# Reordering the slots and the prologue of a fused cross-attention and FP6 layer

## The reference, cut to what matters

```python
# x, ctx: (32, 256, 512) fp32; 16 heads of 32 columns; a causal mask
q = layernorm(x) @ w_q.T + b_q;  k = ctx @ w_k.T + b_k;  v = ctx @ w_v.T + b_v
scores = (q . k) / sqrt(32), -inf above the diagonal
attn = softmax(scores)
x = x + tanh(g_xattn[0]) * ((attn . v) @ w_o.T + b_o)
d = FP6(layernorm(x)), each block of 32 scaled by max|.| / 7.5; w_f likewise
out = x + tanh(g_ffn[0]) * (d @ w_f.T + b_f)
```

## Time and profile before

| | |
|---|---|
| time, median of 3 runs | 1438.02 us (1437.79 to 1441.76) |
| the profiled execution | 1438.69 us, span 1436.9 us |
| TensorE busy | 1361.0 us, 95% |
| VectorE, ScalarE, GpSimd busy | 75%, 69%, 68% |
| mean granted clock of TensorE | 0.986 |
| matmuls | 10333 |

### The profile page before, as it was taken

One profiled execution on the slowest core, in us unless ns is written; L12 is line 12 of the kernel. 1 busy time (PEld: TensorE's weight loads), 2 busy tenths in 40 slices (PEclk: granted clock), 3 DMA queues, 4 the chain that ended last, 5 costly groups with the idle time before them and its releaser, 6 DMA issues.

```text
span 1436.9 us, 33559 instructions
## 1 busy us (share of the span) xinstructions
PE 1361.0 (95%) x10333; PEld 1190.9 (83%) x10333; DVE 1075.8 (75%) x3802; ACT 984.3 (69%) x3101; POOL 975.6 (68%) x1170
## 2 busy tenths in 40 slices
PE   3789999999999999999999999999999999999976
PEld 3678888888888888888888888888888888888854
DVE  2657777877787787778778777777877787787663
ACT  2567777777767777766767777677777767777651
POOL 2347777767767776776777677777767777776662
PEclk9899999999999999999999999999999999999988
DMA  7645656556555665656565565656556565665420
GB/s 205 168 107 123 157 147 168 152 145 174 133 148 149 161 158 144 170 132 149 148 162 152 145 173 126 152 147 168 151 146 174 128 154 142 167 157 130 112 74 30
DMA packets 169544, 209.32 MB, mean 146 GB/s; under 512 B 19084, under 2 KB 84632, under 8 KB 169368
## 3 DMA queue, kind: packets, MB, share of 16 engines
q1 hardware_dynamic: 167640, 204.03, 55.4%
q10 hardware_dynamic: 1728, 3.15, 0.7%
HBM read 72.88 MB, written 33.55 MB: 74 GB/s over the span
## 4 chain that ended last, share of the span: by engine, by line
PE 82%; SPq 5%; DVE 4%; issue 3%; DMA 3%; ACT 1%; POOL 1%; ACTq 0%; DVEq 0%; POOLq 0%
PE proj L527 20%; PE proj L528 18%; PE proj L529 18%; PE pT_ps L583 10%; PE oT_ps L600 7%; SPq L362 5%; PE s_ps L572 5%; PE s_ps L573 2%; DMA stack<-qk 2%; PE proj L627 2%; DVE qk L912 1%; DMA xs<-in_x 1%; POOL all_probs L444 1%; DVE all_probs L965 1%; ACT qk L734 0%
## 5 line engine op out<-in xcount | busy, mean ns | idle before, releaser
L444 POOL TENSOR_TENSOR all_probs<-all_probs,rden 128x256 f32<-128x256 f32 (+1 forms) x512 | 413.2, 828 | 243.6 <-DVE rden L878 239.6
L705 ACT ACTIVATE all_probs<-all_probs,neg_max 128x128 f32<-128x128 f32 (+1 forms) x1024 | 456.1, 447 | 143.4 <-DVE neg_max L870 136.5
L870 DVE CUSTOM_DVE_ANT_0 all_probs<-s_ps,causal 128x128 f32<-128x128 f32 (+1 forms) x1024 | 321.7, 352 | 154.8 <-PE s_ps L573 154.8
L583 PE MATMUL pT_ps<-ident,all_probs 128*128 128x128 f32 x1536 | 213.0, 275 | 6.0 <-POOL all_probs L444 5.9
L583 PEld LDWEIGHTS pT_ps<-ident,all_probs 128*128 128x128 f32 x1536 | 181.6, 142 | 28.3 <-POOL all_probs L444 7.1
L705 ACT ACTIVATION_READ_ACCUMULATOR all_probs<-all_probs,neg_max 128x1 f32 x1024 | 193.3, 189 | 0.0
L734 ACT ACTIVATE qk<-proj,biases 128x256 fp32r<-128x256 f32 x256 | 105.6, 464 | 103.5 <-DMA stack<-qk 96.8
L965 DVE COPY all_probs<-pT_ps 128x384 f32<-128x384 f32 x256 | 141.5, 553 | 32.9 <-PE pT_ps L583 32.9
L527 PE MATMUL proj<-xT_hi,wq_hi 128*128 128x256 f32 x512 | 157.7, 308 | 5.4 <-DVE wq_lo L833 5.4
L527 PE MATMUL proj<-cT_hi,wk_hi 128*128 128x256 f32 x512 | 152.5, 298 | 6.2 <-POOL cT_lo L460 6.2
L572 PE MATMUL s_ps<-stack 96*128 96x256 f32 x512 | 153.5, 300 | 1.0 <-DVE neg_max L870 1.0
(11 more groups left out here) (105 smaller groups left out, 3645.0 us busy)
## 6 DMA issues: line engine op xcount, KB each, us to landing
stack<-qk SPq DMA_DIRECT2D x768, 128.0 KB, 2.5
c_quads<-in_ctx SPq DMA_DIRECT2D x128, 128.0 KB, 3.0
xs<-in_x SPq DMA_DIRECT2D x32, 512.0 KB, 4.4
xn_rows<-xs SPq DMA_DIRECT2D x32, 512.0 KB, 3.0
x_quads<-xn_rows SPq DMA_DIRECT2D x128, 128.0 KB, 3.1
x<-in_x SPq DMA_DIRECT2D x32, 512.0 KB, 4.8
out<-x SPq DMA_DIRECT2D x32, 512.0 KB, 2.8
all_probs<-in_L_xattn_w_k ACTq DMA_DIRECT2D x4, 256.0 KB, 6.2
```

What stands on the lines that cost most here:

```text
L444: last = nc.gpsimd.tensor_tensor(p, p, wide(rden[:, b % 2, t, h:h + 2], (1 + t) * P), ALU.mult)
L583: last = nc.tensor.transpose(pT_ps[h % 2][:, m * P:(m + 1) * P], probs[:, n % P_RING, m * P:(m + 1) * P], ident[:, :])
L705: last = nc.scalar.activation(probs[:, n % P_RING, cols], probs[:, n % P_RING, cols], ACT.Exp, scale=-1.0, bias=neg_max[:, b % 2, t, h:h + 1],
L870: last = nc.vector.tensor_tensor_reduce(probs[:, n % P_RING, cols], s_ps[h % 2][:, cols], causal[:, (1 - t) * P:], 1.0, MASKED, ALU.add, A ...
```

## The change

It has four parts. The first two steps become a prologue (`first`) on every engine, which loads, turns and splits w_k, w_v, w_q, w_o in the order in which they come, with the first units k, v, v, q between them, scales w_f, multiplies b_v with w_o, and issues the first score; the loop then starts at step 2. `biases` grows from 12 to 24 columns, so that the buffers behind it start at multiples of 64 bytes (they started 32 bytes off). Values are weighed at the start of slots 12 and 4 instead of the end of 11 and 3; ScalarE writes oT_hi behind the slot's copy, and VectorE oT_lo in the next slot, behind its maxima. Scores of a head are issued in the middle of the slot before its own. Besides, `SLOT_PARTS` and `AT` have new numbers, and SP issues the next context's quads ahead of x's.

```diff
-AV_SLOTS = (11, 3)
-OUT_SLOTS = (12, 4)
+AV_SLOTS = (12, 4)
-SLOT_PARTS = (2, 4, 2, 1, 2, 4, 2, 4, 2, 4, 2, 1, 2, 4, 2, 4)
+SLOT_PARTS = (2, 4, 2, 4, 1, 3, 2, 4, 2, 3, 2, 4, 1, 4, 2, 2)
 AT = {
-    "cT": ((1, 1), (1, 3)), "cT_hi": ((1, 3), (1, 5)), "cT_lo": ((1, 3), (1, 5)),
-    "moments": ((0, 11), (0, 13)), "rstd": ((0, 12), (0, 14)), "xn": ((0, 13), (0, 15)),
-    "xT": ((1, 5), (1, 5)), "xT_hi": ((1, 5), (1, 6)), "xT_lo": ((1, 5), (1, 7)),
-    "xb": ((3, 3), (3, 7)), "rstd2": ((3, 8), (3, 13)), "y": ((3, 8), (3, 13)), "amax": ((3, 9), (3, 14)),
-    "scales": ((3, 11), (3, 15)), "scaled": ((3, 12), (4, 1)), "grid": ((3, 13), (4, 2)),
-    "xd": ((3, 15), (4, 4)), "xf": ((3, 9), (3, 15)),
+    "cT": ((1, 0), (1, 1)), "cT_hi": ((1, 1), (1, 3)), "cT_lo": ((1, 1), (1, 3)),
+    "moments": ((0, 9), (0, 11)), "rstd": ((0, 10), (0, 12)), "xn": ((0, 11), (0, 15)),
+    "xT": ((1, 3), (1, 6)), "xT_hi": ((1, 5), (1, 7)), "xT_lo": ((1, 5), (1, 7)),
+    "xb": ((3, 3), (3, 7)), "rstd2": ((3, 8), (3, 13)), "y": ((3, 9), (3, 13)), "amax": ((3, 11), (3, 14)),
+    "scales": ((3, 13), (3, 15)), "scaled": ((3, 13), (4, 1)), "grid": ((3, 14), (4, 3)),
+    "xd": ((3, 15), (4, 5)), "xf": ((3, 11), (3, 15)),
 }
+FIRST = [*(("w", "k", m) for m in range(4)), ("k", 0, 0), *(("w", "v", m) for m in range(4)), ("v", 0, 0), ("v", 1, 0),
+         *(("w", "q", m) for m in range(4)), ("q", 0, 0), *(("w", "o", m) for m in range(4))]
+FIRST_STEP = 2
+F_TURNS = {(2, 12): (0, 1), (2, 13): (2, 3)}
+BIAS_COLS = 24
...
-        biases = sb("biases", [P, 3 * KC])
+        biases = sb("biases", [P, BIAS_COLS])
...
@@ SP @@
+            def first():
+                load_c(0)
+                load_x(0)
+                load_rows("v")
+                load_small()
+                load_rows("o")
+                sp.wait_ge(wT_done, whole("k"))
+                load_rows("f")
+                xn_rows(0)
+                load_c(1)
+                xn_quads(0)
+                load_x(1)
+                for t, src in ((add_o, b_o), (add_f, b_f)):
+                    sp.dma_start(t[:, :], across(src)).then_inc(added_in, 16)
+                stack_pair(0, 0)
...
+                if live(i):
+                    load_c(i)
                 if live(i - 1):
-                    sp.wait_ge(xn_out, 16 * i)
-                    if i >= 2:
-                        sp.wait_ge(turned["xT"], 2 * (i - 1))
-                    quads_in(x_quads, xn_dram[(i - 1) % 2], xq_in)
-                if live(i) and i:
+                    xn_quads(i - 1)
+                if live(i):
                     load_x(i)
                 if live(i - 2):
                     stack_pair(i - 2, 1)
-                if live(i) and i:
-                    sp.wait_ge(turned["cT"], 2 * i)
-                    quads_in(c_quads, ctx_in[i], c_in)
                 if live(i - 1):
                     stack_pair(i - 1, 0)
...
@@ TensorE @@
             def step(i):
                 for s in range(SLOTS):
-                    if live(i - 2):
-                        scores(i - 2, s)
+                    for b, r in weighed(i, s):
+                        weigh_values(b, r)
                     units(i, s, 0, SLOT_PARTS[s] // 2)
                     b, h = pair_turned(i, s)
                     if s % 2 == 0 and live(b):
                         transpose_probs(b, h)
                         transpose_probs(b, h + 1)
+                    b, h = (i - 2, s + 1) if s + 1 < SLOTS else (i - 1, 0)
+                    if live(b):
+                        scores(b, h)
                     units(i, s, SLOT_PARTS[s] // 2, SLOT_PARTS[s])
-                    for b, r in weighed(i, s):
-                        weigh_values(b, r)
+            def first():
+                for kind, a, b in FIRST:
+                    if kind == "w":
+                        transpose_weight(TURNED.index((a, b)), a, b)
+                    else:
+                        for part in range(PARTS[kind]):
+                            unit(part, kind, a, b)
+                    if (kind, a, b) == ("k", 0, 0):
+                        transpose_biases()
+                bias_through_o()
+                scores(0, 0)
...
 @@ ScalarE, step(i) @@
-                    for b, r in put_out(i, s):
-                        output_hi(b, r)
...
+                    for b, r in weighed(i, s):
+                        output_hi(b, r)
 @@ VectorE, step(i) @@
+                    for b, r in weighed(i, s - 1):
+                        output_lo(b, r)
                     for unit_ended in ended(i, s):
                         unit(*unit_ended)
...
-                    for b, r in put_out(i, s):
-                        output_lo(b, r)
```

More of the change, by code:

```diff
@@ L92, in live @@
         return 0 <= b < B
-    takers = []
-    for step_no in range(STEPS):
+    takers = [("w", TURNED.index((a, b))) if kind == "w" else (kind, a) for kind, a, b in FIRST]
+    for step_no in range(FIRST_STEP, STEPS):
         for slot_no in range(SLOTS):
@@ L271, in due, with bank_of @@
                     yield i - lag, half
+        def bank_of(kind, half, b):
+            return proj[place_of[kind, 2 * b + half] % BANKS]
         def ended(i, slot):
@@ L277, in ended, with f_chunks @@
                 lag += slot == 0
[L278 to L287 removed]
+                if at_slot == (slot - 1) % SLOTS and part == PARTS[kind] - 1 and live(i - lag) and (
+                        i - (slot == 0) >= FIRST_STEP):
+                    yield kind, half, i - lag, bank_of(kind, half, i - lag)
+        def f_chunks(i, s):
+            for m in F_TURNS.get((i, s), ()):
+                yield TURNED.index(("f", m)), "f", m
         def columns(kind, t):
@@ L311, in weighed @@
                     yield i - 2 - r, r
-        def put_out(i, s):
-            for r, slot in enumerate(OUT_SLOTS):
-                if s == slot and live(i - 2 - r):
-                    yield i - 2 - r, r
         block = es.enter_context(nc.Block())
@@ L406, in step @@
                     sp.dma_start(batch_of(out, b), x1[:, b % 2, :, :]).then_inc(x1_out[b % 2], 16)
-            for i in range(STEPS):
+            first()
+            for i in range(FIRST_STEP, STEPS):
                 step(i)
@@ L783, in weights_to_grid, with first @@
                                      saturate=False).then_inc(w8_ok, 1)
+            def first():
+                load_weight("k")
+                load_weight("q")
+                for t in range(T):
+                    upper("cT", 0, t, cT_hi, ())
+                for m in range(KC):
+                    weight_hi(TURNED.index(("k", m)), "k", m)
+                for t in range(T):
+                    first_norm(0, t)
+                the_biases()
+                unit("k", 0, 0, bank_of("k", 0, 0))
+                for m in range(KC):
+                    weight_hi(TURNED.index(("v", m)), "v", m)
+                the_gates()
+                for half in range(T):
+                    unit("v", half, 0, bank_of("v", half, 0))
+                for t in range(T):
+                    upper("xT", 0, t, xT_hi, ())
+                for m in range(KC):
+                    weight_hi(TURNED.index(("q", m)), "q", m)
+                for m in range(KC):
+                    weights_to_grid(m)
+                unit("q", 0, 0, bank_of("q", 0, 0))
+                for m in range(KC):
+                    weight_hi(TURNED.index(("o", m)), "o", m)
+                bias_v_hi()
+                for t in range(T):
+                    first_norm(1, t)
             def step(i):
-                if i == 0:
-                    for w in "kqv":
-                        load_weight(w)
                 for s in range(SLOTS):
@@ L950, in scales, with first @@
                 nc.vector.reciprocal(blk_inv[:, own], blk_up[:, own]).then_inc(inv_ok, 1)
+            def first():
+                for t in range(T):
+                    turn("cT", 0, t, c_quads, c_in)
+                for t in range(T):
+                    first_moments(0, t)
+                for m in range(KC):
+                    weight_lo(TURNED.index(("k", m)), "k", m)
+                unit("k", 0, 0, bank_of("k", 0, 0))
+                for m in range(KC):
+                    weight_lo(TURNED.index(("v", m)), "v", m)
+                for t in range(T):
+                    turn("xT", 0, t, x_quads, xq_in)
+                weight_scales()
+                for m in range(KC):
+                    weight_lo(TURNED.index(("q", m)), "q", m)
+                unit("q", 0, 0, bank_of("q", 0, 0))
+                for m in range(KC):
+                    weight_lo(TURNED.index(("o", m)), "o", m)
+                for t in range(T):
+                    first_moments(1, t)
+                bias_v_lo()
+                added()
             def step(i):
```

118 lines of the change are left out of this document (48 added, 70 removed), and 4 rows, old and new, of the table WEIGHT_TURNS.

## The result

The kernel after takes 1544.2 us (median of 4 runs, 1533.81 to 1546.12). The ratio to before is 1.0721, 95% interval 1.0667 to 1.0775: 106 us slower, where 30 were forecast and a range that ended at 1488. The direction was right, the size was not. The profiled execution's span is 1544.0 us, its mean granted clock 0.954 (0.986 before).

What follows compares the result with a forecast made beforehand. TensorE, busy 95% of the span, was taken as the bound. Steady steps +1.4 us times 29 (+40.6), start of step 2 -1, step 2 -13, step 3 +1, tail +2.4: together +30, so 1468 us, range 1408 to 1488.

Steps and rivals of the forecast that it cites:

- rival C: Slot 3: VectorE also waits for x quads issued behind the context's; 1.0 us a step on top of A, 1497 us; chance 0.10.
- A: Main forecast: TensorE waits for oT_lo before unit o in each step; 1468 us, own range 1445 to 1480; chance 0.56.
- Unit o's wait: Before unit o's first part: the low half needs 3.16 us against 1.6 of cover, so +1.55 us a step.
- Unit f0's wait for dT_lo: Unit f0, beginning in slot 3, waits 0 to 0.3 us for its low half; taken as +0.2 us a step.
- The wait ahead of the weighing: TensorE's idle time before the weighing (L600) mostly goes with its later place: -0.45 us a step, bounds 0 and 0.9.
- Scores half a slot ahead: Scores straight behind transposes eight times a step cost up to 0.03 us each; taken as +0.1 us a step.
- The prologue: First two steps: step 2 begins 1 us earlier, bounds 5 either way; step 2 itself takes 38 us for 51.3, minus 13.
- Step 3: The step with unit o but no f0, forecast 1 us longer.
- Alignment: Buffers at multiples of 64 bytes: no gain in the sum, bounded by 4% of a step's stream, 1.1 us.
- B: Unit o: the low half is there in time and the wait does not show; 1414 us; chance 0.27.
- D: Whole kernel: gains and losses cancel with unit o's wait near 0.55 us; 1434 to 1442 us; chance 0.04.
- E: TensorE's streams: alignment speeds them up, bound 1.1 us a step, turning A's 1468 into 1436 us; chance 0.03.

Runs made afterwards that it cites:

- e2: The kernel after with SP's old order in the loop, x's quads ahead of the next context's: 1464.22 us, ratio 1.0169 to before.
- e5: The kernel after with eight more 512-column matmuls before the first o matmul of each batch but the first: 1515.06 us, ratio 1.0514 to before.
- e4: The kernel after with both the old SLOT_PARTS and SP's old order: 1411.96 us, ratio 0.9805 to before.
- e1: The kernel before with only the 24 columns for biases, so later buffers lie at multiples of 64 bytes: 1433.88 us, ratio 0.9960.
- e11: e4 with the weighing back at the ends of slots 11 and 3 and its evacuations at their old places: 1410.88 us, ratio 0.9780 to before.
- e10: e4 with the scores put back to the start of their slot: 1418.50 us, ratio 0.9837 to before.
- e9: The kernel before with only the new prologue and the 64-byte multiple: 1429.53 us, ratio 0.9915.
- e7: The kernel after with VectorE's xT turns back in slot 5 and ScalarE's second xT_hi in slot 6: 1463.18 us, ratio 1.0166 to before.

## Why the prediction was wrong, step by step

**The step that failed is rival C's: the x quads behind the context's.** The prediction saw the mechanism and its marks (issue later in the step, VectorE's cols waiting, maxima, copy, q1 and oT_lo behind), gave it 0.10, and put it at nothing in the sum. It cost 2.6 us a step in place of C's 1.0, 80 us in all, and only the part that is waiting was in C's price. Three things in it were too kind:

- The quads were reckoned at 11.2 us into the step and are there at 12.5: issued at 7.2, not 6.6, with the landing 3.7 us in the median, not 3.1. VectorE wanted them at 9.7, not 8.9. The gap of 2.3 us that I had worked out came to 2.8. My own numbers thus already gave a wait of 2.3 us. What talked me out of it was one clause, that the turn fits in VectorE's wait for the transposes. That is true of the turn's 1.1 us, but not of the wait before it, during which the maxima that ScalarE wants, and through it oT_hi, stand still.
- The price, 0.4 to 1.8 us a step, was right for the waits alone: TensorE's idle time is 1.25 us a step above e2's. e5, where the clock is at 1.00, lies 44.41 - 42.90 = 1.5 us a step above e2 (an upper reading, since it holds some of the fill).
- The clock had no term at all. TensorE's waits were of 1.8 to 4.2 us, and 21 of 28 brought a stretch at 1.2 GHz: 1.35 us a step against e2, and at least 1.08 against e5. The kernel before has clock 0.87 in its window 51:102 with 11.3 us of idle time, so the row that prices it had been read, for the prologue only.

**The steps that held**, to be read in e2, which is the kernel after without C: it takes 1.0169 of before, 1462 us, where A had 1468. A steady step there is 1.01 us above before, where the sum had 1.4, and the first steps and the tail are dearer than forecast, so the closeness of the two times is in part luck.

- *Unit o's wait* is 1.42 us (1.55). oT_lo starts 791.77 - 789.38 = 2.4 us behind the end of the weighing in e2 (worked out: 3.16 - 0.68 - 0.14 = 2.34). Against e4 the new shares cost 1.52 us a step (unit o's and f0's waits together, 1.75).
- *Unit f0's wait for dT_lo*: 4.9 us in 24 times, 0.2 us each (0.2).
- *The wait ahead of the weighing*: gone, but the size fits by luck. e4's step is 0.51 us shorter than before (-0.45), of which only 0.26 is idle time (6.8 us in the steady state for 14.4); the other 0.25 is busy time, about what e1 shows for the 64-byte multiple. And by e11 that wait is nearly gone without the later place, with the early scores and the new `AT`.
- *Scores half a slot ahead* was set at 0.1 us of cost and is, if anything, a gain (0.18 us a step, e10 against e4).
- *The prologue.* Step 2 starts 3.3 us later, within the bounds of 5 but on the other side; step 2 has 37.4 us in e2 (38), of which the prologue alone gives 42.8 (e9) and the order within the step the rest. It has 41.9 only with C, whose wait of 4.8 us at 66.28 stands in front of slot 3's maxima.
- *Step 3* was forecast at +1 and has +7.6: C again (6.36 us of wait, the longest of all); e2 has 41.56, +3.2, because the quads are late in this step even with SP's old order (VectorE waits 3.26 us for them at 103.50, and TensorE 5.03 us for oT_lo at 107.87). With the turn in slot 5 that wait is 2.27 us and the step has 38.0 (e7).
- *Alignment*: nothing in the sum, and 5 us in e1. That "the stream rates stand as they are" did not hold: the spacing of 512-column matmuls fell from 0.233 to 0.229 us. The prediction's estimate by the Trainium skill's spacing ("TensorE: Matmul & The Clock Gate", Back-to-back issue gap) is worked out wrong: its own terms, 28.4 us x (1 - 0.216 / 0.237), make 2.5 us a step, not 1.9. Nothing in the sum rests on it, and no run came down to 0.216 us.
- *Tail*: +1.2 (+2.4) in the kernel after, +3.3 in e2.

**B and D** are ruled out: the wait is there and shows. **E** as priced is ruled out too, though a quarter of its bound is real. That e4's 1412 us lies at B's 1414 is a coincidence: e4 has the old shares, so its low half comes in time by the old cover, and half of its gain a step is faster streams, which B did not have.

**What stays open.** How much of e2's step is due to the new `AT` times alone was not tried. Nor was the exact share of the clock: e5 adds work, so its 1.08 us a step is a lower bound, and the 35 us by which the same 9281 instructions are longer in the steady state are another reading (1.2 us a step against before, 1.35 against e2), since waits move too. Why the clock fell at 21 of the 28 waits and not at the other seven is not explained.

## What to carry to other kernels

Where an edit moves a transfer past another in its queue, work out when it lands and when the consumer gets to it, and if the difference is positive, put it into the sum in full: an in-order engine that waits for late data also holds what stands behind it, here maxima, a copy and an evacuation that TensorE needed. Late data is harmless where it is wanted late (e7 gave back all 80 us by moving two turns). On a kernel that is full, price each new wait of TensorE twice, once as idle time and once as a stretch at half clock that may come with it: here waits of 1.42 us cost no clock, and longer ones mostly did. Look at busy time and idle time apart: a faster stream can end in a longer wait, as in e1, and pay only when the wait is taken away. Try the parts of a bundle apart: here two of its parts cost 9% together, and the others gain 2%.

## What the hardware showed that was not expected

- In the window 797.4:802 of the kernel after, the granted clock is 0.63 behind 1.9 us of idle time in 5.4 us, and 1.00 before and after. In e2, TensorE idles 1.42 us once a step, 25 times, at a clock of 1.00 throughout. Over the steady state of after, 69 us of added idle time came with 35 us of slower work.
- Dummy work in a wait made a kernel faster: e5 has eight extra matmuls (some 1.9 us) in each step of the steady state and takes 29 us less than the kernel after.
- 32 bytes of offset in buffers that are not the weights cost TensorE 2% in the spacing of its 512-column matmuls (0.233 us, 0.229 without the offset). The kernel gained only 0.4% from their going (e1), since TensorE waited longer elsewhere. Why the offset costs is not known.
